# Two graph layers on one core: pair tables and w2 rows by DMA, finer waits at the begin, and DVE's turned rows in one operation per quad

## The reference, cut to what matters

```
h = relu(layernorm(x)); x = x + L0(h, adj); h = relu(layernorm(x)); x = x + L1(h, adj)

L0:  D = |x_i - x_j| for all pairs           (64, 128, 128, 128)
     h = D @ W1.T + b1                       (64 outputs per pair)
     h = leaky(batchnorm over all pairs(h)); s = h @ W2.T
     s = where(adj > 0, s, -9e15); A = softmax(s)
     y = leaky(batchnorm((A @ x) @ Wg.T + bg)); out = [x, y] @ Wt.T + bt
L1:  h = x @ W; e = leaky(h@a1 + (h@a2)^T), masked by adj, softmax over axis 1
     out = elu(attention @ h)
```

## Time and profile before

| | before |
|---|---|
| median of three runs | 1115.59 us |
| the profiled execution | 1117.84 us |
| its span, first to last instruction | 1115.8 us |
| granted clock of TensorE, mean | 0.992 |
| PE busy | 1043.5 us (94%) |
| DVE busy | 1040.2 us (93%) |
| ACT busy | 1000.5 us (90%) |
| POOL busy | 611.3 us (55%) |
| begin, to PE's first product | 0 to 22.45 us |
| chain that ended last | PE 46%, ACT 21%, DVE 21% |

### The profile page before, as it was taken

How to read it: one execution, slowest core, us unless ns; L and a number is a source line. 1 busy time by engine, 2 the same in 40 slices (tenths; PEclk the granted TensorE clock), 3 DMA queues, 4 the chain that set the end, 5 groups by cost and what they waited for, 6 DMA issues and landing times.

```text
span 1115.8 us, 17336 instructions
## 1 busy us (share of the span) xinstructions
PE 1043.5 (94%) x6278; PEld 450.6 (40%) x6278; DVE 1040.2 (93%) x1382; ACT 1000.5 (90%) x1268; POOL 611.3 (55%) x347
## 2 busy tenths in 40 slices
PE   3999999999999999999999989999999999888897
PEld 1433333333333333333333332233333333257786
DVE  5899999999999999999999988899999999968897
ACT  4889998999999899999999979999999999944897
POOL 6587678778777777877777720232143242321430
PEclk9999999999999999999999989999999999999999
DMA  6444443454444344444445479999999999952012
GB/s 185 148 155 188 159 179 154 170 196 173 181 180 175 153 170 191 176 180 179 174 170 196 174 301 379 354 343 317 331 331 320 330 326 326 329 160 55 21 58 76
DMA packets 99059, 233.30 MB, mean 209 GB/s; under 512 B 9120, under 2 KB 46464, under 8 KB 98976
## 3 DMA queue, kind: packets, MB, share of 16 engines
q1 hardware_dynamic: 86704, 219.97, 54.1%
q0 software_dynamic: 2240, 7.34, 1.9%
q10 hardware_dynamic: 10032, 4.89, 1.6%
HBM read 124.43 MB, written 107.74 MB: 208 GB/s over the span
## 4 chain that ended last, share of the span: by engine, by line
PE 46%; ACT 21%; DVE 21%; issue 9%; POOL 2%; ACTq 1%; DMA 0%; DVEq 0%; POOLq 0%
PE psum L818 19%; ACT store L705 15%; PE psum L828 11%; PE psum L832 8%; DVE store L298 6%; DVE plain_st L1148 3%; ACT store L624 1%; POOL store L298 1%; PE psum L934 1%; PE psum L808 1%; PE psum L790 1%; DVE bst L1335 1%; DVE early L1281 1%; DVE rows L1280 1%; DVE bst L1297 1%
## 5 line engine op out<-in xcount | busy, mean ns | idle before, releaser
L298 POOL TENSOR_TENSOR store<-h_ext 128x2048 f32<-128x2048 f32 (+1 forms) x96 | 386.5, 4028 | 99.4 <-PE psum L818 95.5
L818 PE MATMUL psum<-store,w1tt_sb 128*64 128x512 f32 x1792 | 424.5, 600 | 11.8 <-ACT store L624 10.8
L298 DVE TENSOR_TENSOR store<-psum,h_ext 128x2048 f32<-128x2048 f32 x160 | 363.6, 2272 | 1.0 <-ACT h_ext L594 1.0
L624 ACT ACTIVATE store<-store 128x2048 f32<-128x2048 f32 x160 | 305.8, 1929 | 17.4 <-DVE store L298 11.7
L705 ACT ACTIVATE store<-store,st 128x1024 f32<-128x1024 f32 x192 | 227.2, 1241 | 0.0
L818 PEld LDWEIGHTS psum<-store,w1tt_sb 128*64 128x64 f32 x1792 | 123.1, 137 | 253.1 <-issue 229.7
L828 PE MATMUL psum<-store,w_twice 128*64 128x512 f32 x768 | 201.6, 602 | 6.6 <-DVE early L1205 3.5
L1148 DVE BATCH_NORM_STATS2 plain_st<-store 128x6 f32<-128x512 f32 x256 | 160.3, 676 | 0.0
L832 PE MATMUL psum<-early 128*64 128x512 bf16 x1152 | 158.9, 382 | 0.0
L298 DVE TENSOR_TENSOR store<-h_ext 128x2048 f32<-128x2048 f32 x64 | 147.5, 2305 | 6.5 <-PE psum L818 6.5
L636 ACT COPY store<-psum 128x1024 f32<-128x1024 f32 x128 | 128.5, 1025 | 16.7 <-PE psum L818 11.6
(11 more groups left out here) (164 smaller groups left out, 1084.2 us busy)
## 6 DMA issues: line engine op xcount, KB each, us to landing
kept_products<-store SPq DMA_DIRECT2D x192, 512.0 KB, 2.9
store<-kept_products SPq DMA_DIRECT2D x192, 512.0 KB, 5.9
early<-score_skew POOLq DMA_DIRECT2D x14, 384.0 KB, 6.4
early<-adj SPq DMA_DIRECT2D x16, 256.0 KB, 3.5
early<-adj_t SPq DMA_DIRECT2D x16, 256.0 KB, 3.6
store<-x ACTq DMA_DIRECT2D x16, 256.0 KB, 6.0
out<-early SPq DMA_DIRECT2D x16, 256.0 KB, 2.3
score_skew<-early POOLq DMA_DIRECT2D x14, 128.0 KB, 5.4
```

Source lines behind the costliest of these rows:

```text
L298: return engine.tensor_tensor(t[:, :, 0:steps, :], nodes.unsqueeze(2).broadcast_to([C, 2, steps, N]), windows(h_ext[:, 2 * c, :], STEP * m ...
L624: nc.scalar.activation(t, t, ACT.Abs).then_inc(abs_ready, 1)
L818: last = nc.tensor.matmul(t[MID * g:MID * g + MID, b, :], w1tt_sb[:, 0:MID], diff[slot][:, g, b * BANK:b * BANK + BANK], start=True, stop= ...
```

## The change

- POOL's three additions for the tables and minus_ident are gone. The host makes the table (nodes_in, 128 x 1536 words of 4 bytes, 786 KB), and SP loads it third. w2_rows comes by DMA too (w2_in, 131 KB), and ACT's 16 copies are gone.
- ACT's queue issues two loads, ident and w1. The others go to SP's queue, in this order: x groups 0 and 1, the table, three maps (fold, l1_wt, col), x group 2, adj, x groups 3 and 4, six weights with w2. In place of weights_in for nine there are w1_in, maps_in, nodes_here and weights_in, each waited for where it is used first.
- Group 1's statistics and scales (and POOL's power for it) stand ahead of the loop over chunks, behind the doubling of w1.
- For quad 0 `rest` writes its result in place, in PSUM, and `middle` and y_split read it there. PE waits for y_split ahead of chunk 2 in place of y_rested.
- LOAD_X issues 3, 5, 4 and 4 pieces at 257, 262, 268 and 272 in place of 8, 4 and 4 at 257, 262 and 268.
- take_turned is one operation of 256 columns for the whole quad; last_mask is four times as wide.

```diff
-STAT_AT = (None, 1, 13, 60, 140)
-POWER_AT = (None, 2, 15, 63, 143)
-SCALE_AT = (None, 2, 18, 70, 150)
+STAT_AT = (None, None, 13, 60, 140)
+POWER_AT = (None, None, 15, 63, 143)
+SCALE_AT = (None, None, 18, 70, 150)
...
-        last_mask = sb("last_mask", [128, DIST])
+        last_mask = sb("last_mask", [128, QUAD, DIST])
...
+        def rest_tile(u):
+
+            return y_rest[:, :] if u > 0 else y_tile(0)
...
-        LOAD_X = {257: range(0, 8), 262: range(8, 12), 268: range(12, NQ)}
+        LOAD_X = {257: range(0, 3), 262: range(3, 8), 268: range(8, 12), 272: range(12, NQ)}
...
+            load_group(0)
+            load_group(1)
+            sp.dma_start(early[:, 1024:1024 + WIDE // 2 * len(MAXED)], nodes_in).then_inc(nodes_here, 16)
+            for t, src in ((fold, fold_in), (l1wt_sb, l1_wt), (col, cols)):
+                sp.dma_start(t[:, :], src).then_inc(maps_in, 16)
+            load_group(2)
             load_adj(0)
+            load_group(3)
+            load_group(4)
+            for t, src in ((wg_sb, wg_t), (wt1_sb, wt1_t), (wt2_sb, wt2_t), (l1w_sb, l1_w), (bt_sb, bt_rows),
+                           (w2_rows.rearrange("p r q -> p (r q)"), w2_in)):
+                sp.dma_start(t[:, :], src).then_inc(weights_in, 16)
...
-            pool.wait_ge(ident_here, 32)
-            pairs_of(0)
-            pairs_of(1)
             deviation(0)
-            for k in range(2, len(MAXED)):
-                pairs_of(k)
+            deviation(1)
...
-                nc.scalar.copy(y_part(u, 1), by_couple(y_rest[:, :])).then_inc(y_mid, 1)
+                nc.scalar.copy(y_part(u, 1), by_couple(rest_tile(u))).then_inc(y_mid, 1)
...
-            act.wait_ge(weights_in, 16 * 9)
-            act.wait_ge(consts_set, 1)
-            for r in range(8):
-                for g in range(2):
-                    c, s = divmod(r, 4)
-                    at = 4 * (2 * c + g) + s
-                    last = nc.scalar.copy(w2_rows[MID * g:MID * g + MID, r, at:at + 1],
-                                          col[MID * g:MID * g + MID, 3:4])
-            last.then_inc(w2_set, 1)
+            act.wait_ge(maps_in, 16 * 3)
...
                 if n == 2:
-                    pe.wait_ge(y_rested, 1)
+                    pe.wait_ge(y_split, 1)
...
-                        pe.wait_ge(nodes_ready, MAXED.index(n) + 1)
+                        pe.wait_ge(nodes_here, 16)
...
             for n in range(QUAD):
                 graph_statistics(n)
             statistics(0)
             scales(0)
-            dve.wait_ge(weights_in, 16 * 9)
+            dve.wait_ge(w1_in, 16)
             nc.vector.tensor_scalar(w1_twice[:, :], w1tt_sb[:, 0:MID], 2.0, None, ALU.mult).then_inc(weights_made, 1)
             for n in range(QUAD, 2 * QUAD):
                 graph_statistics(n)
+            statistics(1)
+            scales(1)
...
-                turned_rows = att[1].rearrange("p d (q m) -> p d q m", q=4)
-                in_order = lambda t: t.rearrange("p (r q d) -> p r q d", r=4, q=4)
-                for b in range(QUAD):
-                    last = nc.vector.tensor_tensor(in_order(s_turn[:, b, :]),
-                                                   turned_rows[:, :, :, 4 * b:4 * b + 4].rearrange("p d q r -> p r q d"),
-                                                   in_order(last_mask[:, :]), ALU.mult)
-                last.then_inc(turn_ready, 1)
+                in_order = lambda t: t.rearrange("p b (r q d) -> p (b r) q d", r=4, q=4)
+                nc.vector.tensor_tensor(in_order(s_turn), att[1].rearrange("p d (q m) -> p d q m", q=4)[:, :, :, 0:16].rearrange("p d q m -> p m q d"),
+                                        in_order(last_mask[:, :, :]), ALU.mult).then_inc(turn_ready, 1)
```

More of the change, by code:

```diff
@@ L87, in two_layers @@
 def two_layers(nc, x, adj, adj_t, w1_tt, wg_t, wt1_t, wt2_t, l1_w, l1_wt, cols, bt_rows,
-               ident_in, minus_in, fold_in, out):
+               ident_in, nodes_in, w2_in, fold_in, out):
     kept_dram = nc.dram_tensor("kept_products", [NKEPT, 128, WIDE], F32, kind="Internal").ap()
@@ L185, in two_layers @@
                psum[:, 5, :].rearrange("p (b n) -> p b n", b=QUAD)]
-        weights_in, ident_here = sem("weights_in"), sem("ident_here")
+        weights_in, maps_in, w1_in, ident_here, nodes_here = (sem(n) for n in (
+            "weights_in", "maps_in", "w1_in", "ident_here", "nodes_here"))
         x_in = [sem(f"x_in{g}") for g in range(len(GROUPS))]
@@ L190, in two_layers @@
             "dve_ln", "var_ready", "rstd_ready", "scale_ready", "h_ready", "turned", "h_ext_ready"))
-        consts_set, wa_ready, weights_made, nodes_ready, w2_set = (sem(n) for n in (
-            "consts_set", "wa_ready", "weights_made", "nodes_ready", "w2_set"))
+        consts_set, wa_ready, weights_made = (sem(n) for n in ("consts_set", "wa_ready", "weights_made"))
         y_mm, y_high, y_rested, y_mid, y_split = (sem(n) for n in (
@@ L390, in _, with load_group @@
         def _(sp):
-            for g, (a, b) in enumerate(GROUPS):
+            def load_group(g):
+                a, b = GROUPS[g]
                 sp.dma_start(h_nat[:, QUAD * a:QUAD * b, :], x_n[:, QUAD * a:QUAD * b, :]).then_inc(x_in[g], 16)
@@ L464, in _ @@
             nc.gpsimd.memset(sums_st[:, :, :], 0.0)
[L465 to L471, removed]
+            nc.gpsimd.memset(last_mask[:, :, :], 1.0).then_inc(consts_set, 1)
             def deviation(g):
@@ L577, in _ @@
             act.dma_start(ident[:, :], ident_in).then_inc(ident_here, 16)
-            act.dma_start(minus_ident[:, :], minus_in).then_inc(ident_here, 16)
-            for t, src in ((w1tt_sb, w1_tt), (l1wt_sb, l1_wt), (col, cols), (wg_sb, wg_t),
-                           (wt1_sb, wt1_t), (wt2_sb, wt2_t), (l1w_sb, l1_w), (bt_sb, bt_rows), (fold, fold_in)):
-                act.dma_start(t[:, :], src).then_inc(weights_in, 16)
+            act.dma_start(w1tt_sb[:, :], w1_tt).then_inc(w1_in, 16)
             def normalise(u):
@@ L812, in _ @@
             turn(0)
-            pe.wait_ge(weights_in, 16 * 9)
+            pe.wait_ge(w1_in, 16)
             node_products(0)
@@ L1204, in _ @@
                     dve.wait_ge(y_mid, 1)
-                    nc.vector.tensor_tensor(y_part(0, 2), by_couple(y_rest[:, :]), y_part(0, 1), ALU.subtract).then_inc(y_split, 1)
+                    nc.vector.tensor_tensor(y_part(0, 2), by_couple(rest_tile(0)), y_part(0, 1), ALU.subtract).then_inc(y_split, 1)
                 for lag, kinds in ((LAG_COUNT, PLAIN), (LAG_COPY, COPIED)):
@@ L1416 @@
     node = np.arange(128)
+    apart = (STEP * np.array(MAXED)[:, None] + 1 + np.arange(STEP)).reshape(-1, 1)
+    ends = (node == node[:, None, None]) | ((node + apart) % N == node[:, None, None])
+    nodes = np.where(ends, 0xBF80, 0).astype(np.uint16).reshape(128, -1)
+    w2_rows = np.zeros((128, 8, 32), np.float32)
+    for r in range(8):
+        for g in range(2):
+            w2_rows[MID * g:MID * g + MID, r, 4 * (2 * (r // 4) + g) + r % 4] = a["L0_gnn_W2"][0]
+    w2_rows = w2_rows.reshape(128, -1)
     arrays = {
@@ L1423 @@
         "ident_in": np.eye(128, dtype=np.float32),
-        "minus_in": -np.tile(np.eye(128, dtype=np.float32), 2)[:, :EXT],
+        "nodes_in": nodes.view(np.float32), "w2_in": w2_rows,
         "fold_in": (node[:, None] % MID == node[None, :] % MID).astype(np.float32),
```

13 lines of the change are left out of this document (7 added, 6 removed).

## The result

The changed kernel takes 1105.95 us (median of four, 1103.98 to 1108.12) against 1115.58 before: 9.6 us less, a ratio of 0.9911 with a 95% interval of 0.9899 to 0.9924. The forecast said 1104.4.

What follows compares the result with a forecast made beforehand. It took a serial chain to bound the begin, PE pass 1, an ACT-DVE loop pass 2. Begin 7.25, wide turn 2.3 and x loads 1.6 sum to 11.15 us; 1115.59 less that is 1104.4, range 1101.0 to 1109.0.

Steps and rivals of the forecast that it cites:

- Begin: Start of the kernel up to PE's first product: 7.25 us gained (5.75 plus 1.5), PE starting at about 15.2.
- The three stalls: At the begin, three DVE 128x4 operations under POOL's table additions: 2.02, 2.09, 2.13 us would become 0.16 each, saving 5.75.
- Rival C: At the begin, PE reaches its higher level sooner: first chunk 3 us, not 6.0, so 1101.4 us; chance 0.07.
- Moved statistics: At the begin, group 1's statistics ahead of DVE's first difference cost nothing, as DVE was idle; some 0.5 us of cover.
- rival B: At the begin, POOL's difference holds group 1's scale up to 4.18 us; begin gains 3.1, total 1108.6; chance 0.08.
- Tables: At the begin, the table by DMA lands at about 7.5 us, is wanted at 15.2, and so costs nothing.
- rival D: At the begin, the table lands late, PE starts at about 22.2, begin gains 0.25: 1111.4 us; chance 0.05.
- Wide turn: In pass 2, one 0.42 us operation for four taking 0.61: 0.19 a quad, 2.3 us over 12 quads.
- Rivals A and E: Pass 2: A, it doesn't shorten, 1106.7 us, chance 0.16; E, wide operation pays for its 64 runs, slower, chance 0.03.
- x loads: End of pass 2: three loads, not eight, ahead of quad 14's exponential gain 1.6 us; bounds 0 and 3.1.
- the rest of the chain there shifts with it: End of pass 2: the table of half scores and last sum move earlier with the normalisation, keeping the 1.6 us.
- fewer loads run beside the store: End of pass 2: fewer x loads would run beside the skewed store; no size given.

Runs made afterwards that it cites:

- after_again: The changed kernel run once more, unaltered, on another chip: 1107.03 us, ratio 0.9907 to the kernel before.
- warm_pe: The changed kernel with x loads issued 2, 2, 6, 6 and unread identity matmuls in PE's waits at begin and change of passes: 1100.74 us, ratio 0.9857.
- four_turns: The changed kernel with the wide operation undone, four operations of 64 columns put back: 1107.76 us, ratio 0.9912 to the kernel before.
- begin_as_before: The kernel before with only the wide turn and the new order of x loads, its begin kept: 1113.81 us, ratio 0.9970.

## Why the prediction was right

The time, 1105.95, is 1.5 us above 1104.4 and within 1101.0 to 1109.0. The waits named in the forecast were there, and went where it said; the parts are of about its sizes.

- **Begin** (7.25 us, PE at 15.2): exact in place (15.20, 15.19). The three stalls (5.75) went and came back with two-input work on POOL; the moved statistics were worth 1.5 when undone, as worked out, and the PSUM place holds off 0.7. What the sum left out is PE's level, read from the durations: the first chunk took 6.0 us before, 5.6 in after_again and 4.4 in after, so that 8.5 us were gained at chunk 3 in one trace, 7.7 in the other. Rival C had this in kind, but not its bound: with PE at the higher level from the start (warm_pe) the first chunk took 3.0 us, but ACT ended the wait behind it, so the 3 us it promised aren't there.
- **Moved statistics** at no cost: right, 0.7 us of cover; rival B didn't come. **Tables** at no cost: right, the table was issued at 1.75 and took 6.7 us to land, 8.4 against 15.2; rival D didn't come.
- **Wide turn** (2.3 us; 0.42 each): 0.416 us, and over quads 0 to 12 2.36 us (before to after), 1.9 when undone (four_turns) and 2.75 with the old begin (begin_as_before against before), one trace each. Rivals A and E fell. The rule of the Trainium skill's page "VectorE: DVE Perf Modes" (section on the TRN2 errata) would have had 4.5 us. The trace after disagrees: four operations in 0.61 us became one of 0.416, 0.19 us a quad, where the rule has 0.77 and 0.39.
- **x loads** (1.6 us): 1.29 in the trace, 1.09 with after_again. The fold waited for its load as forecast (1.13 us, in after_again 1.66, before 1.57), and the normalisation gained 2.06. The step that was off is "the rest of the chain there shifts with it": quad 15's scores take 11.4 us through DRAM with eight loads of x beside them, and they now end the wait. The forecast's sentence that fewer loads run beside the store came to nothing, as all eight did. Undoing the loads costs 1.7 to 1.9 us in the chain of one trace.
- **The sum against the median**: 11.15 forecast, 13.6 between two traces, 9.6 between the medians; 10.35 between the medians on the chip of after_again. The forecast took the trace of before for its median plus a constant 2.25 us, which would have put the profiled execution at 1106.7; it came at 1103.98. The traces of before and after_again differ by 11.4 us, nearly the sum, but from other parts: 7.7 at the begin, 0.7 on the way to quad 0, of which the forecast says nothing, 2.3 in the quads and 1.1 at the end of pass 2, less 0.3 behind it. That the total lies so close is in part luck: these offsets, and up to 2 us of chance in each trace, could have added up. How the remaining 1.5 us of the median come about is not settled: no trace of a median run of either kernel on that chip is there to compare.

## What to carry to other kernels

Look for small operations of DVE that take several times what the same line takes elsewhere: their ends, set beside POOL's, tell what holds them, and an input moved to PSUM, or POOL's table made elsewhere, sets them free. Where one path sets a period of near-full engines, an overhead of 0.2 us on that path counts in every round, though the engine's busy share hardly shows it. When transfers are put off to free a queue, ask what travels beside them at the new time: here splitting eight loads freed ACT's exponential, but the trip of the scores got shorter only when fewer loads went with it.

## What the runs showed of the hardware that was not expected

- POOL's two-input operation holds DVE's operation with two SBUF inputs to its own end (0.67, 1.86, 1.85, 1.41 us; 1.12 us for y_split, which ends 0.3 behind it). The hold goes both ways: in pass 2 of the kernel before, POOL's L537 took up to 2.2 us in place of 0.73 beside DVE's L298, and DVE's next one-input bit mask 1.64 in place of 1.23.
- A one-input operation on POOL held four of DVE's for 0.82, 1.00, 0.37 and 0.36 us and let others through. The Trainium skill's page "GPSIMD Engine Reference" (specifications) names DVE's two inputs and its 2-port mode as what contends. L1103, with one input, may be of the second kind; that L1108 and L1106, with two, come free in the middle of POOL's operation isn't explained.
- By its durations PE came to its higher level at 18.1 us in one run of the changed kernel and after 20 in the next, with the same work at the same times (15.20 and 15.19), which moved the chunk after it by 0.8 us. The granted clock of the view read 1.00 all the while.
- 18 matmuls on the identity in PE's waits kept the granted clock at 1.00 over the change of passes, where it had been at 0.5 for 7 to 10 us, and shortened the way to quad 0 by 1.6 to 2.3 us; about 0.5 of it was lost again in the quads, and no gain of the whole kernel is shown.
- The skewed scores took 10.5 to 11.8 us through DRAM and back with eight loads of 256 KB issued in the first 7 us, and 8.6 to 9.8 with four.
